# The experts' rows by transposing DMA instead of TensorE transposes, with a rearranged front part

## The reference

```python
decay = exp(-exp(w)) * (0.5 + 0.5 * tf)          # per channel; tf is a gate per batch
a_t = a_{t-1} * decay + exp(k_t) * v_t           # and b_t the same with exp(k_t); forward and backward
out = sigmoid(r) * num / den * (0.8 + 0.2 * tf)
# middle layer: mixes of h and the shifted h, then
x = x + (sigmoid(r) * sigmoid(k + u) * v) @ Wout   # first half, r, k, v = mixes @ Wr, Wk, Wv
x = x + sigmoid(r2) * (relu(k2) ** 2 @ cWv)         # second half
# experts: 32 experts in 4 groups, 8 for each token, hidden size 256, latent size 256
latent = x @ fc1.T
y = sum_j weight_j * (relu(latent @ w1[e_j].T) ** 2 @ w2[e_j].T)   # e_j: the token's 8 experts
out = x + y @ fc2.T + relu(x @ up.T) ** 2 @ down.T
```

## Time and profile before

| | |
|---|---|
| median of 3 runs | 1173.27 us (1172.0 to 1175.05) |
| profiled execution, its time | 1163.3 us |
| its span, first to last instruction | 1161.6 us |
| mean granted TensorE clock | 0.979 |
| TensorE busy | 1065.5 us (92%) |
| VectorE, ScalarE, GpSimd busy | 693.9, 511.9, 574.5 us |

### The profile page before, as it was taken

One profiled execution on the slowest core, in us unless ns is written; L12 is line 12 of the kernel. 1 busy time (PEld: TensorE's weight loads), 2 busy tenths in 40 slices (PEclk: granted clock), 3 DMA queues, 4 the chain that ended last, 5 costly groups with the idle time before them and its releaser, 6 DMA issues.

```text
span 1161.6 us, 13472 instructions
## 1 busy us (share of the span) xinstructions
PE 1065.5 (92%) x4102; PEld 644.4 (55%) x4103; DVE 693.9 (60%) x1307; ACT 511.9 (44%) x770; POOL 574.5 (49%) x449
## 2 busy tenths in 40 slices
PE   0479999999999999599999999999999999999938
PEld 0334344444434444354544444448999999999914
DVE  8996559999999999641785000004444444444335
ACT  3465435666566646231212111106566565665401
POOL 3524015513552456200027777754777777777720
PEclk9989999999999999799999999999999999999959
DMA  4553024524551527211205666276888788788695
GB/s 153 176 188 97 1 37 134 163 80 123 167 160 49 161 101 214 68 30 72 73 21 188 243 216 213 104 257 142 137 137 143 137 140 142 135 141 142 86 249 213
DMA packets 126033, 157.72 MB, mean 136 GB/s; under 512 B 8992, under 2 KB 104224, under 8 KB 125984
## 3 DMA queue, kind: packets, MB, share of 16 engines
q1 hardware_dynamic: 94688, 113.63, 32.7%
q0 software_dynamic: 31296, 43.53, 19.9%
HBM read 79.67 MB, written 77.46 MB: 135 GB/s over the span
## 4 chain that ended last, share of the span: by engine, by line
PE 63%; DVE 27%; issue 6%; DMA 1%; ACT 1%; POOL 1%; POOLq 0%; ACTq 0%; DVEq 0%; SPq 0%
PE banks L613 12%; PE banks L544 12%; PE banks L624 11%; PE banks L1613 10%; PE banks L567 9%; DVE arena L1477 3%; DVE arena L1381 3%; PE banks L600 3%; DVE arena L1372 3%; DVE arena L1370 3%; PE banks L522 2%; DVE arena L1389 2%; DVE arena L1413 2%; DVE arena L1399 2%; PE banks L1640 1%
## 5 line engine op out<-in xcount | busy, mean ns | idle before, releaser
L1613 PE MATMUL banks<-arena 128*128 128x512 f32 x896 | 389.7, 595 | 8.6 <-DVE arena L1480 5.6
L1613 PEld LDWEIGHTS banks<-arena 128*128 128x128 f32 x896 | 170.7, 191 | 224.4 <-issue 219.1
L484 POOL DMA_INDIRECT sums<-arena x160 | 249.5, 1559 | 84.5 <-DVE arena L874 57.2
L472 POOL DMA_INDIRECT slots_in<-arena x128 | 129.2, 1009 | 91.3 <-issue 86.9
L874 DVE TENSOR_TENSOR arena<-banks,arena 128x512 f32<-128x512 f32 x80 | 55.3, 692 | 172.2 <-PE banks L624 172.2
L613 PE MATMUL banks<-arena 128*128 128x128 f32 x1280 | 156.1, 275 | 1.3 <-ACT arena L713 1.3
L624 PE MATMUL banks<-arena 128*128 x640 | 151.1, 379 | 0.0
L613 PEld LDWEIGHTS banks<-arena 128*128 128x128 f32 x1280 | 149.3, 192 | 1.8 <-issue 1.7
L544 PE MATMUL banks<-arena 128*128 128x512 f32 x320 | 145.0, 601 | 0.7 <-ACT arena L740 0.7
L624 PEld LDWEIGHTS banks<-arena 128*128 128x128 f32 x640 | 115.6, 190 | 12.5
L713 ACT ACTIVATE arena<-arena 128x512 f32 x160 | 91.9, 622 | 52.1 <-issue 51.4
(11 more groups left out here) (178 smaller groups left out, 1259.8 us busy)
## 6 DMA issues: line engine op xcount, KB each, us to landing
slots_in<-arena SPq DMA_DIRECT2D x20, 1120.0 KB, 6.0
arena<-slots_in SPq DMA_DIRECT2D x80, 280.0 KB
arena<-fT SPq DMA_DIRECT2D x32, 256.0 KB, 3.0
arena<-w2T SPq DMA_DIRECT2D x4, 2048.0 KB, 13.3
arena<-sums SPq DMA_DIRECT2D x16, 512.0 KB, 8.7
sums<-arena SPq DMA_DIRECT2D x4, 1152.0 KB, 5.6
arena<-xT SPq DMA_DIRECT2D x4, 1024.0 KB, 8.2
arena<-xT POOLq DMA_DIRECT2D x4, 1024.0 KB, 9.1
```

Source lines behind the costliest of these rows:

```text
L472: pool.indirect_dma_start(rows_in, bass.IndirectOffsetOnAxis(ap=POSU[:, n, j:j + 1], axis=0), XLR[:, n], None).then_inc(S['scattered'], 16)
L484: pool.indirect_dma_start(sums[g % RING], bass.IndirectOffsetOnAxis(ap=DESTU[:, g:g + 1], axis=0), YO[:, i % 4, c], None, compute_op=ALU.add)\
L1613: ins = pe.matmul(out, w[:, k, m * P:(m + 1) * P], x[:, k], start=(k == 0), stop=(k == kt - 1))
```

## The change

The experts' rows: GpSimd scatters rows of which `rows` has split each latent word into its low and its high half word, first all 256 low ones, then all 256 high ones. SP loads the metadata (24 words a row) and the latent part of a pair by two DMAs; the second is a transposing one on half words, 256 rows x 512 half words to 128 partitions x 4 groups x 256 (`PLANES`: a plane of low and one of high half words). VectorE's `xT` copies the planes to `XTB` and interleaves them back to words. `t1` is gone; the ring waits for `xT_copied`. The last pairs on TensorE are written out in another order, and 12 matmuls of ones come after the second load of the sums.

The front part: sigmoid(r) stays in its PSUM bank, and VectorE makes the product of the two gates (`product`) in place of GpSimd's `gate_product`; PSUM banks are assigned in another order (`O_BANK`, `mix_banks`); the first mix is handed to TensorE tile by tile (`by_tiles`), `y_stage` of batch 0 likewise; residuals are grouped (0, 1, 2), (3); in the last batch the residuals come between the item's forward scan and its `back`, `center` before the numerator's `back`, and `x_sides` after the bonus; the last `fin` comes after `mixes`.

```diff
-O_BANK = (0, 1, 3, 4)
+O_BANK = (1, 4, 0, 3)
 def mix_banks(b):
-    return dict(k2=(0, 1, 3, 4), r2=(2, 7, 0, 1), v2=(3, 4, 2, 7))
+    return dict(k2=(1, 4, 0, 3), r2=(2, 7, 1, 4), v2=(0, 3, 2, 7))
...
-XTB = place(2, 2, KL, P)
+XTB = place(2, KL, 2 * P)
-XGB = place(4, 2, ROW)
+META = place(4, 2, ROW - LAT)
+PLANES = place(4, KL * 2 * P).bitcast(U16).rearrange("p q (h k s) -> p q h k s", h=2, k=KL)
...
 def ld(sp, dst, name):
-def pair(dram, i):
-    return dram[bass.ds(2 * i, 2)].rearrange("c p d -> p c d")
-def xg_load(sp, i, q, h):
-    if not (isinstance(i, int) and i < 4):
-        sp.wait_ge(S['t1_mm'], i - 3)
+def xg_load(sp, i):
+    q = i % 4
+    if i >= 4:
+        sp.wait_ge(S['xT_copied'], i - 3)
-        sp.sem_inc(S['sp_settled'], 1)
-    sp.dma_start(XGB[:, q], pair(slots_in, i)).then_inc(S[f'xg_loaded{q}'], 16)
+    rows = slots_in[2 * i:2 * i + 2]
+    sp.dma_start(META[:, q], rows[:, :, LAT:ROW].rearrange("c p d -> p c d")).then_inc(S[f'xm_loaded{q}'], 16)
+    sp.dma_start_transpose(PLANES[:, q].rearrange("p h k s -> p (h k) s"),
+                           rows.rearrange("c p d -> (c p) d").bitcast(U16)[:, 0:2 * LAT])\
+      .then_inc(S[f'xg_loaded{q}'], 16)
...
-    for i in range(4):
-        xg_load(sp, i, i, 0)
-    with sp.Fori(0, NP // 4 - 1) as h:
-        for q in range(4):
-            xg_load(sp, 4 * h + q + 4, q, h)
+    for i in range(NP):
+        xg_load(sp, i)
...
 def rows(dve, tiles):
-        dve.tensor_copy(XLR[:, n, 0:LAT], bank(FG_BANK[n])[:, 0:LAT]).then_inc(S['rows_copied'], 1)
+        planes = XLR[:, n, 0:LAT].bitcast(U16).rearrange("p (h l) -> p h l", h=2)
+        dve.tensor_copy(planes, bank(FG_BANK[n])[:, 0:LAT].bitcast(U16).rearrange("p (l h) -> p h l", h=2))\
+           .then_inc(S['rows_copied'], 1)
...
-    def t1(i, q, h):
-        pe.wait_ge(S[f'xg_loaded{q}'], 16 * h + 16)
-        if not (isinstance(i, int) and i < 2):
-            pe.wait_ge(S['xT_copied'], i - 1)
-        for c in range(2):
-            for k in range(KL):
-                ins = pe.transpose(bank(q % 2)[:, (c * KL + k) * P:(c * KL + k + 1) * P],
-                                   XGB[:, q, c, k * P:(k + 1) * P], IDENT)
-        ins.then_inc(S['t1_mm'], 1)
...
-                                    w[:, k, m * P:(m + 1) * P], XTB[:, q % 2, c, k],
+                                    w[:, k, m * P:(m + 1) * P], XTB[:, q % 2, k, c * P:(c + 1) * P],
...
-            if not (last and q > 1):
-                at(t1, 2)
-            if not (last and q > 2):
-                at(m1, 1)
+            at(m1, 1)
-    t1(0, 0, 0)
-    t1(1, 1, 0)
-    four(0, True, False)
+    four(0, True)
-        four(h, False, False)
-    four(NP // 4 - 1, False, True)
-    m2(NP - 1, 3, NP // 4 - 1, experts(NP - 1))
+        four(h, False)
+    h, i = NP // 4 - 1, NP - 4
+    known = experts(i - 1)
+    m1(i + 1, 1, h)
+    m2(i - 1, 3, h - 1, known)
+    known = experts(i), experts(i + 1)
+    m1(i + 2, 2, h)
+    m2(i, 0, h, known[0])
+    m2(i + 1, 1, h, known[1])
+    known = experts(i + 2), experts(i + 3)
+    m1(i + 3, 3, h)
+    m2(i + 2, 2, h, known[0])
+    m2(i + 3, 3, h, known[1])
+    pe.wait_ge(sums_loaded[0][1], 16)
+    for n in range(3 * TT):
+        pe.matmul(bank(0)[:, n % TT * P:(n % TT + 1) * P], ones, ones, start=True, stop=True)
...
     def xT(i):
-        dve.wait_ge(S['t1_mm'], i + 1)
+        dve.wait_ge(S[f'xg_loaded{i % 4}'], 16 * (i // 4) + 16)
-        dve.tensor_copy(XTB[:, i % 2].rearrange("p c k s -> p (c k s)"), bank(i % 2)).then_inc(S['xT_copied'], 1)
+        dve.tensor_copy(XTB[:, i % 2].bitcast(U16).rearrange("p k (s h) -> p h k s", h=2), PLANES[:, i % 4])\
+           .then_inc(S['xT_copied'], 1)
     def meta(i):
+        at_w, at_pos, at_token = IN_META
+        dve.wait_ge(S[f'xm_loaded{q}'], 16 * (i // 4) + 16)
-        step.did(dve.tensor_tensor(EQW[:, q % 2], XGB[:, q, :, AT_POS:AT_POS + TOPK], places, ALU.is_equal))
-        dve.tensor_copy(DESTU[:, mine].rearrange("p (c o) -> p c o", o=1), XGB[:, q, :, AT_TOKEN:AT_TOKEN + 1])
+        step.did(dve.tensor_tensor(EQW[:, q % 2], META[:, q, :, at_pos], places, ALU.is_equal))
+        dve.tensor_copy(DESTU[:, mine].rearrange("p (c o) -> p c o", o=1), META[:, q, :, at_token])
-        step.did(dve.tensor_tensor(EQW[:, q % 2], EQW[:, q % 2], XGB[:, q, :, AT_W:AT_W + TOPK], ALU.mult))
+        step.did(dve.tensor_tensor(EQW[:, q % 2], EQW[:, q % 2], META[:, q, :, at_w], ALU.mult))
...
-    def gate_product(b, m):
-        pool.wait_ge(S['k_evac'], 4 * b + m + 1)
-        if m == 0 and b > 0:
-            pool.wait_ge(S['o_mm'], 4 * b)
-        pool.tensor_tensor(PROD[:, m], SRt, SKt, ALU.mult).then_inc(S['gates_ready'], 1)
-    FIRST, USUAL = {2: (0,), 3: (1,), 4: (2, 3)}, {0: (1,), 1: (2, 3)}
-    def slots(items, following, b=None, gates={}, adds=False):
+    def slots(items, following, b=None, late=False):
+        if b is not None:
+            add_x(b - 1)
-            if adds and n == 0:
-                add_x(b - 1)
-            early = gates is USUAL and n == 1
-            if not early:
-                for m in gates.get(n, ()):
-                    gate_product(b, m)
-            if adds and n == 7 and following is not None:
-                gate_product(b + 1, 0)
-            late = not adds and n == 3 and gates is FIRST
-            if nx is not None and not late:
+            last = late and n == len(items) - 1
+            if nx is not None and not last:
-            if early:
-                for m in gates.get(n, ()):
-                    gate_product(b, m)
-            if late:
+            if last:
-        for m in gates.get(len(items), ()):
-            gate_product(b, m)
-        if adds:
+        if b is not None:
...
     def gate_r(b, m):
-        act.wait_ge(S['gates_ready'], 4 * b + m)
+        if 4 * b + m >= 2:
+            act.wait_ge(S['r_evac'], 4 * b + m - 1)
-        act.activation(SRt, bank(RKV[m % 2][0]), ACT.Sigmoid).then_inc(S['r_evac'], 1)
+        act.activation(bank(RKV[m % 2][0]), bank(RKV[m % 2][0]), ACT.Sigmoid).then_inc(S['r_sig'], 1)
     def gate_k(b, m):
-        act.activation(SKt, bank(RKV[m % 2][1]), ACT.Sigmoid, bias=tmu[:, m:m + 1]).then_inc(S['k_evac'], 1)
+        act.activation(SIGS[:, m % 2], bank(RKV[m % 2][1]), ACT.Sigmoid, bias=tmu[:, m:m + 1]).then_inc(S['k_evac'], 1)
...
-            square(2, b)
+        square(2, b)
-        if not nxt:
-            square(2, b)
...
     def product(b, m):
-        dve.wait_ge(S['gates_ready'], 4 * b + m + 1)
+        if m == 0 and b > 0:
+            dve.wait_ge(S['o_mm'], 4 * b)
+        dve.wait_ge(S['r_sig'], 4 * b + m + 1)
+        dve.wait_ge(S['k_evac'], 4 * b + m + 1)
+        dve.tensor_tensor(PROD[:, m], SIGS[:, m % 2], bank(RKV[m % 2][0]), ALU.mult).then_inc(S['r_evac'], 1)
+        dve.wait_ge(S['r_evac'], 4 * b + m + 1)
     def y_stage(b, ks=range(K)):
-            if k == 0:
-                dve.wait_ge(S['fin_done'], K * (b + 1) if b < 2 else 8 * b - 3)
+            if b == 0:
+                dve.wait_ge(S['fin_done'], k + 1)
+            elif k == 0:
+                dve.wait_ge(S['fin_done'], 2 * K if b == 1 else 8 * b - 3)
...
-            first = FIRSTB[:, MIXES.index(name)].rearrange("p (k o) -> p k o", o=1)
-            ins = dve.tensor_tensor(out[:, :, 0:1], out[:, :, 0:1], first, ALU.add)
+                if by_tiles(which, b, n):
+                    ins = dve.tensor_tensor(out[:, k, 0:1], out[:, k, 0:1], column(FIRSTB, name, k), ALU.add)
+                    if k < K - 1:
+                        ins.then_inc(S['mix_tile'], 1)
+            if not by_tiles(which, b, n):
+                first = FIRSTB[:, MIXES.index(name)].rearrange("p (k o) -> p k o", o=1)
+                ins = dve.tensor_tensor(out[:, :, 0:1], out[:, :, 0:1], first, ALU.add)
...
         if nxt:
             slot(items[7], settle_second)
         else:
-            slot(items[7])
-            x_sides(b - 1)
-            fin(items[7])
+            it = items[7]
+            fwd(it)
             for n in range(2):
                 residuals(b, n)
+            dve.wait_ge(S['fwd_done'], it['i'] + 1)
+            back(it, 1).then_inc(S['bwd_done'], 1)
+            fin(it['prev'])
             center(2, b)
+            back(it, 0)
+            bonus_den(it)
+            bonus_num(it)
+            x_sides(b - 1)
         return items[7]
     def residuals(b, n):
-        if n < 2:
-            residual(b, 2 * n)
-            residual(b, 2 * n + 1)
+        for m in ((0, 1, 2), (3,), ())[n]:
+            residual(b, m)
     chain(first_items, second_items[0])
     items = chain(second_items, body_items(1)[0])
...
-    slot(items[0], lambda: y_stage(0))
+    y_stage(0, range(K - 1))
+    slot(items[0], lambda: y_stage(0, (K - 1,)))
...
-    iteration(B - 1, False, before)
+    final_item = iteration(B - 1, False, before)
+    fin(final_item)
...
-            if m == 0:
+            by = by_tiles(1, b, n) and m == 0
+            if m == 0 and not by:
```

(13 more changed lines are left out.)

25 lines of the change are left out of this document (13 added, 12 removed).

## The result

| | before | after |
|---|---|---|
| first chip, median | 1174.16 us (1172.0 to 1177.67, 4 runs) | 1157.99 us (1157.37 to 1160.2, 4 runs) |
| second chip, median | 1162.48 us (1161.53 to 1164.43, 13 runs) | 1145.92 us (1144.61 to 1147.26, 4 runs) |
| ratio, first chip | | 0.9863, 95% interval 0.9834 to 0.9891 |
| ratio, second chip | | 0.9861, 0.9844 to 0.9877 |

The change makes the kernel 16 us faster, where I had forecast 34. The level differs by 12 us between the two chips, for both kernels alike, and the ratio doesn't. The profile shown here is the first one of the changed kernel: time 1158.06 us, span 1156.3.

What follows compares the result with a forecast made beforehand. TensorE paced the experts' loop at 3.95 us a pair, with GpSimd next at 3.72. Loop -17, front -3, last batch -11 and tail -3 gave -34 from 1173.3: 1139.3, stated as 1140 us, range 1127 to 1238.

Steps and rivals of the forecast that it cites:

- the floor of 3.72 us a pair: Experts' loop: GpSimd's two scatters of 1.56 us, each with 0.30 us of issue, allow no shorter period.
- the front as a whole: Part before the experts' loop: -3 us net from moving gate products to VectorE, -11 us in the last batch.
- the last batch: Front part: reordered work fills VectorE's waits, -12.7 us, dearer rows' copies add 1.6; -11 us, between -6 and -13.
- the other batches: Front part: 16 gate products on VectorE cost +12.5 us, stalls against GpSimd worth 15 us go; net -3 us.
- 159 steps of 1.86 us are 295.7: Experts' loop, first to last scatter: paced by GpSimd it takes 295.7 us instead of 312.9, a gain of 17 us.
- an occasional hit 1145 to 1160: Loop: mild form of the rival that VectorE's new copy blocks GpSimd's scatters; 1145 to 1160 us, rival's chance 0.15.
- The full hold: Loop: same rival's strong form, each copy delays a scatter by its whole length; period 4.40, time 1194 us, rival's chance 0.15.
- the DMA term: Loop: the transposing load's cost to the DMA engines, taken as 1.6 us a pair, fitting with 0.2 to spare.
- The limit of 1.83 us: Loop: DMA time left for the load in a 3.72 us pair, with the scatters at 1.89.
- the rivals of a dear load: Loop: DMA engines become the bound, moderately (1146 to 1250 us, chance 0.30) or far dearer (1428 at high bound, 0.17).
- my own case: Loop paced by GpSimd, the load hidden: 1127 to 1152 us, chance 0.38.
- the tail: After the loop: added matmuls of ones before latent(0) make twelve matmuls take 5.3 us instead of 7.93; with transposes -3 us.

Runs made afterwards that it cites:

- the OR from PSUM: Changed kernel with VectorE's copy of half words made an OR with zeros lying in PSUM: 1135.99 us, 0.9762 of before.
- the second profile of after: Changed kernel profiled once more with no edit: span 1142.9 us, median 1145.92 us, 0.9861 of before.
- the front alone: Kernel before with only the change's front part, experts' loop as before: 1149.13 us, 0.9889 of before.
- another 256 KB a pair: The OR from PSUM plus one more DMA per pair, copying the pair's 256 KB from DRAM to DRAM: 1136.82 us, 0.9786 of before.
- the plain load: Changed kernel with a non-transposing load of the same 256 KB, copy of half words kept: 1146.57 us, 0.9856 of before.
- the word copy: The plain load with rows not split and VectorE copying 512 words instead of 1,024 half words: 1135.01 us, one run.
- the OR from PSUM and 24 ones: The OR from PSUM with 24 matmuls of ones ahead of the tail instead of 12: 1134.14 us, 0.9758 of before.

## Why the prediction was partly wrong

**Right.** The direction; that GpSimd becomes the loop's bound and its gaps are 0.30 us of its own issue; the floor of 3.72 us a pair, which the OR from PSUM reached (3.73); the front as a whole, -14 forecast and -13.4 measured alone, nearly all of it the last batch (-11 forecast, -12.0 measured); the -3 of the other batches, a price of 12.5 us against 15 us of stalls by estimate, can't be told from the difference between executions. What a row can show of the front is as forecast. Source lines of after: the product with the gate, the operation that was held up to 1.25 us, and the copies of the rows:

```profile
L1416 DVE TENSOR_TENSOR arena<-arena,banks x16: 678/679/686, 90.0 to 417.0; 128x512 f32<-128x512 f32 x16
```

```profile
L1472 DVE TENSOR_TENSOR arena<-arena x19: 151/156/159, 78.8 to 501.6; 128x4 f32<-128x4 f32 x19
```

```profile
L538 DVE COPY arena<-banks x16: 677/680/692, 490.9 to 553.5; 128x512 uint16<-128x512 uint16 x16
```

The 16 products cost 0.68 us each as assumed. L1472 is at 0.16 us throughout. The rows' copies went from 0.413 to 0.680 us, as priced, and of the 1.6 us that I charged 0.8 or so remain (from the first product of the back part, L525, to the last evacuation before the loop it is 299.5 us in the second profile of after and 298.7 with the front alone). In the last batch TensorE's wait of 12.59 us is gone: the mean runs at 471.84 us in 3.60 us instead of 6.07.

**Wrong: the length of the scatters.** The step that failed is "159 steps of 1.86 us are 295.7". It took the scatter's 1.56 us over unchanged; with VectorE's copy beside it the mean is 1.64, and (1.644 - 1.559) x 159 = 13.5 us of the missing 18 are that (308.6 - 295.7 = 12.9 in the second profile). The mechanism stood among the rivals, at 0.15, with "an occasional hit 1145 to 1160" as its mild form. What I held against it was wrong evidence: the operations of L861, 162 ns beside scatters that keep 1,559, told nothing of a longer copy, while the 5.10 us scatter beside the 5.52 us operation was the nearer row, SBUF to SBUF and long, though with two inputs. The full hold (4.40 us a pair) was wrong too: the copy holds GpSimd at the scatter's start and near its end only, in this profile by at most 0.53 us (2086 - 1557 ns) of 0.74 and mostly by 0.13. The Trainium skill (SBUF — State Buffer, "Who interferes with whom") says that VectorE in a two-port mode and GpSimd block each other fully, for the whole instruction, and that an operation with at most one SBUF input outside these modes leaves GpSimd alone. The traces agree with the second, 1559 ns beside the OR, and with the first in part: the scatters are longer, 1635 ns, but a copy that begins 0.09 us into a scatter costs it nothing and takes its usual 0.74 us. In which mode the copy ran no row shows.

**Wrong in its reasoning, though near in size: the DMA term.** I called the load's price "the term that decides", took 1.6 us and left 0.2 to spare. It is 1.77 us in after and, with the OR, 54.9% of 3.73, 2.05 us, which with the scatters' 2.01 (53.8%) is more than the period; still the period is 3.73. The limit of 1.83 us didn't exist: the shares of two queues can't be added up against the period. With another 256 KB a pair the loads' queue rose to 72.8%, the scatters' fell from 53.8 to 48.9, and the period stayed. So the rivals of a dear load, 0.47 of my chances, went by a sum that decides nothing here, and my own case used the same sum. Against the plain load the transposing costs 0.47 us of the engines' time a pair (1.77 and 1.30) and nothing of the kernel's, 1145.92 and 1146.57 us.

**Unsteady: the tail.** -3 was forecast; the two profiles of after give -1.4 and -3.6 against before's (51.2 and 50.7 us from the last scatter to the end), and the medians with and without ones differ by 1.9 us at most. The condition that I named, that the ones run until `latent(0)` is ready, holds in one profile of the two, and the quicker transposes come in four of all ten with 12 ones.

**The level.** I put the 10 us between before's profile and its median on the result. On the chips where before runs at 1162.5 us the sum should have been made without them: the changed kernel takes 1146 us there, 17 above 1162.5 - 34 = 1128.5. Of these 17, 13 are the scatters. The other 4 aren't placed: the tail differs by 2.7 us between two executions of the same kernel, and in batch 0 the second norm of the same front part starts anywhere from 147.3 us (the word copy) to 150.3 (after).

The kernel with the OR from PSUM and 24 ones has the lowest time of those tried, 1134.14 us, 0.9758 of before (0.9745 to 0.9772), though its interval overlaps with those of the OR with 12 ones and with none.

## What to carry to other kernels

When GpSimd's indirect DMAs set the pace, look at which of VectorE's operations read and write only SBUF, and whether they run at a scatter's start or near its end: here a form with an operand in PSUM was 0.5 us longer than the copy and made the kernel 10 us faster. Read a price of interference from the longest row of its kind in the trace, not from short operations that had no chance to collide. A DMA share near 1.0 from several queues is no proof that the engines are full: ask whether anything waits for a landing.

## What was not expected of the hardware

- A scatter of 1.56 us is lengthened by VectorE's SBUF-to-SBUF copy of 0.74 us when the copy runs at its start, or begins 0.52 to 1.24 us into it and ends at 1.60 us or after; a copy that begins 0.05 to 0.35 us into it costs nothing, and of six that began at 0.51 to 0.53 us in the two profiles five cost 0.13 to 0.15. Where the scatter came first, the copy was the one to wait, up to 1.10 us instead of 0.74.
- The DMA engines' summed share reached 1.22 of the time at 218 GB/s, and the loop's period stayed at 3.735 us.
- A transposing DMA of 256 half-word rows of 512 takes SP 1.23 us to issue, against 0.37 for a plain one, and about 1,300 packets with its metadata instead of 272; both hide here.
- Both kernels are 12 us slower on one chip than on others; the one profile of the changed kernel from there has a stretch of 14 us in which ScalarE waits 12.46 us, and the profiles from the other chips don't.
